# First attention of a four-part macaron block: state growth and A x V of the tile in front issued ahead of the scores, use of the state behind them

## The reference

```
qkv = x @ Wqkv_w.T + Wqkv_b ; k = k * SCALE ; g = sigmoid(gamma_raw)      # 16 heads of 16
for each position t of a sequence of 1024:
    state = g * state + v_t k_t^T          # 16 x 16 for each head
    y_t   = state @ q_t
x = x + y @ out_w.T + out_b
```

## Time and profile before

| | us |
|---|---|
| median of 3 runs | 2789.87 |
| profiled execution, whole time | 2792.29 |
| profiled execution, span | 2790.3 |
| first attention, from about 564 to 1018 | 454 |
| TensorE busy in these 454 | 407.6 |

### The profile page before, as it was taken

The page is one execution under the profiler, slowest core; times in us unless marked ns, Lnnn a source line. Parts: engine busy times, 40 slices in busy tenths (PEclk is TensorE's granted clock), DMA queues, the critical chain, the costliest instruction groups (busy, mean ns, idle before and its releaser), DMA issues.

```text
span 2790.3 us, 75964 instructions
## 1 busy us (share of the span) xinstructions
PE 2565.9 (92%) x31464; PEld 2148.2 (77%) x31464; DVE 1795.8 (64%) x4190; ACT 1369.6 (49%) x2281; POOL 1146.1 (41%) x1382
## 2 busy tenths in 40 slices
PE   4999999989989969999999899988999999969998
PEld 3888788777777757877887688877888888848887
DVE  7887788445655558888876466554656656545554
ACT  4444444244444424434443577765444544427776
POOL 5555555333333325555554333311443443453332
PEclk9999999899999989999999999999999999989999
DMA  5000000000110010000000000000000000000001
GB/s 174 1 6 1 1 1 1 1 18 22 22 22 22 22 46 1 1 1 1 1 1 1 17 1 1 1 9 19 17 17 18 17 17 18 19 1 23 31 31 38
DMA packets 67557, 45.85 MB, mean 16 GB/s; under 512 B 13184, under 2 KB 66192, under 8 KB 67216
## 3 DMA queue, kind: packets, MB, share of 16 engines
q1 hardware_dynamic: 67216, 41.00, 5.4%
HBM read 15.78 MB, written 8.40 MB: 9 GB/s over the span
## 4 chain that ended last, share of the span: by engine, by line
PE 25%; issue 13%; POOL 11%; DVE 8%; ACT 6%; SPq 0%; DMA 0%; POOLq 0%; DVEq 0%; ACTq 0%
PE ps L591 5%; PE ps L46 3%; PE ps L48 3%; PE ps L47 3%; PE ps L246 2%; PE ps L1373 2%; ACT XN L234 2%; DVE st L203 2%; POOL rs L219 2%; PE ps L1374 2%; POOL a1pry L1943 2%; POOL a1pry L1945 2%; POOL a1l L1931 2%; ACT gHf L1413 2%; DVE XTL L256 1%
## 5 line engine op out<-in xcount | busy, mean ns | idle before, releaser
L591 PE MATMUL ps<-WDT,fHT 128*128 128x256 f32 (+1 forms) x1536 | 386.0, 394 | 8.7 <-ACT fHT L642 8.7
L591 PEld LDWEIGHTS ps<-WDT,fHT 128*128 128x128 f32 (+1 forms) x1536 | 283.4, 192 | 82.4 <-issue 42.8
L1438 DVE TENSOR_TENSOR gHl<-gHf,gHh 128x512 fp32r<-128x512 f32 x256 | 180.6, 707 | 256.3 <-ACT gHh L1417 256.1
L720 POOL TENSOR_TENSOR fV<-fH,frc 128x704 f32<-128x704 f32 x128 | 178.3, 1393 | 339.3 <-DVE frc L709 339.3
L46 PE MATMUL ps<-WGH,XTH 128*128 128x512 f32 (+1 forms) x768 | 312.6, 407 | 2.4 <-DVE XTL L256 1.4
L48 PE MATMUL ps<-WGL,XTH 128*128 128x512 f32 (+1 forms) x768 | 289.0, 376 | 0.0
L47 PE MATMUL ps<-WGH,XTL 128*128 128x512 f32 (+1 forms) x768 | 288.5, 376 | 0.0
L1388 PE MATMUL ps<-W2T,gHh 128*128 128x256 f32 x1024 | 257.8, 285 | 0.0
L1390 PE MATMUL ps<-W2T,gHl 128*128 128x256 f32 x1024 | 255.1, 281 | 0.0
L234 ACT ACTIVATE XN<-X,nb,rs 128x256 f32<-128x256 f32 x384 | 198.8, 589 | 69.0 <-POOL nb L223 69.0
L1373 PE MATMUL ps<-XTH,W1T 128*128 128x512 f32 x512 | 208.9, 408 | 18.9 <-DVE XTL L256 16.4
(11 more groups left out here) (225 smaller groups left out, 6386.6 us busy)
## 6 DMA issues: line engine op xcount, KB each, us to landing
X<-in_x SPq DMA_DIRECT2D x16, 512.0 KB, 8.9
a0vp<-a0vt SPq DMA_DIRECT2D x256, 32.0 KB, 1.9
a1vp<-a1vk SPq DMA_DIRECT2D x256, 32.0 KB, 2.2
out<-X SPq DMA_DIRECT2D x16, 512.0 KB, 2.9
tws<-in_w SPq DMA_DIRECT2D x2, 1024.0 KB, 7.6
WN<-in_wgu SPq DMA_DIRECT2D x3, 384.0 KB, 6.1
a0km<-in_wqkv SPq DMA_DIRECT2D x2, 384.0 KB, 3.2
a1pry<-in_aw SPq DMA_DIRECT2D x1, 768.0 KB, 4.9
```

Source lines behind the costliest of these rows:

```text
L591: h = pe.matmul(down, HT[n % 2][0:m, c, :], WDT[0:m, c, :], start=(c == 0), stop=(c == 5))
L1438: dve.tensor_tensor(Hl[m % 8][:, :], Hf[m % 4][:, :], Hh[m % 8][:, :].bitcast(F32), ALU.subtract).then_inc(s_hl, 1)
```

## The change

Tile `n` on PE was v(n), S(n), E(n-1), V(n-1), G(n), O(n-2). It becomes v(n), G(n-1), V(n-1), S(n), E(n-1), O(n-2). G thus moves one tile later in the numbering, V moves ahead of S, and E stays behind S. Since V is now the first to write bank 6, its matmuls start the group and E's end it; V waits for ACT's copy of the tile in front (`s_ye`) and ACT's copy waits for both V and E (`s_av` and `s_it`). The ring follows the new order. On DVE the state updates of tile `n-1` stand ahead of the decays of tile `n`. In tile 0 only v and S remain, and the wait for the end of the feed-forward (`s_xd`) stands in tile 1.

```
@@ slots0
             for n in range(NT + 2):
                 if n < NT:
-                    yield from [("v", n), *[("s", n, q) for q in range(4)]]
-                    if n % 8 < 7:
-                        yield ("u", n)
+                    yield ("v", n)
+                if 0 < n <= NT and (n - 1) % 8 < 7:
+                    yield ("u", n - 1)
+                if n < NT:
+                    yield from [("s", n, q) for q in range(4)]
@@ attn0_pe: enter, values
             def enter(m):
 
-                if m:
-                    pe.wait_ge(s_ye, m)
...
-                                              start=(k == 0 and (h == 0 or m % 8 == 0)), stop=False,
-                                              skip_group_check=True)
+                                              start=False, stop=True, skip_group_check=True)
...
             def values(m):
+
+                if m:
+                    pe.wait_ge(s_ye, m)
...
-                                          a0A[m % 2][:, 256 * q + c:256 * q + c + 64], start=False, stop=True,
-                                          skip_group_check=True)
+                                          a0A[m % 2][:, 256 * q + c:256 * q + c + 64],
+                                          start=(h == 0 and k == 0), stop=False, skip_group_check=True)
@@ attn0_pe: the loop over tiles
+                if n == 1:
+                    pe.wait_ge(s_xd, NT)
+                if 0 <= m < NT:
+                    grow(m)
+                    values(m)
                 if n < NT:
                     scores(n)
-                if n == 0:
-                    pe.wait_ge(s_xd, NT)
                 if 0 <= m < NT:
                     enter(m)
-                    values(m)
-                if n < NT:
-                    grow(n)
@@ attn0_act
                 if m >= 0:
                     act.wait_ge(s_av, m + 1)
+                    act.wait_ge(s_it, entered(2 * m + 1))
@@ attn0_dve
                 i, j = n // 4, n % 4
+                if 0 < n <= NT:
+                    state(2 * n - 2)
+                    if (n - 1) % 8 < 7:
+                        state(2 * n - 1)
                 if n < NT:
                     decay(n)
-                    state(2 * n)
-                    if n % 8 < 7:
-                        state(2 * n + 1)
```

## The result

Thirteen runs of the changed kernel gave 2800.94 to 2815.93 us with a median of 2812.35; thirteen of the kernel before, on the same chips, 2782.69 to 2801.63 with a median of 2793.47. The ratio is 1.0067, with a 95% interval of 1.0054 to 1.0080: the change makes the kernel 0.67% slower, some 19 us. The forecast was 2795, +5 us, with a range from 2783 to 2806. The sign was right, the size was not.

A forecast was written before the change was run, and what follows sets the result against it. Chains over ACT and POOL, not PE, were taken as the bound. Boundaries +10.4, absorption -5.2, start -1, end +1 gave +5.2 us on 2792.29, so 2797.5; less 2.4 to the median, 2795, range 2783 to 2806.

The forecast's parts named there:

- G's waits go, V's and S's come: PE's waits: G's for POOL gone, V's for the DMA from 2.9 to 20 us or more, S's some 10 us.
- The chain at an ordinary boundary, +0.74 us: Tiles 47 to 49: S waits 0.75 us, V 1.0, then V 1.1; the chunk gets 0.74 us longer.
- L: Time from the end of `Vt` to the landing of its DMAs; taken as 4.1 us, low 3.7, high 5.7.
- The clock at nothing: TensorE's granted clock: no term in the sum; half clock after the new waits only in a rival of chance 0.12.
- A half should be absorbed afterwards: The 14 chunks: half of 0.73 us a chunk, lost to single PE events, absorbed; -5.2 us, ends 0 and -10.
- The start, -1 us: Tile 0: K's transposes no longer stand behind G's 3.86 us wait, but V(0) waits for its DMAs; -1 us.
- The end, +1 us: Tiles 60 to 63, no projection behind O: S and E now stand behind V's DMA waits; +1 us.
- the new waits cost clock: Rival, chunk boundaries: three shorter waits lower the clock in 10 more boundaries, +10 on top of +5, 2807; chance 0.12.
- PE becomes the bound: Rival: V hardly waits for DMAs, G's waits go, S's 0.75 us comes at 15 chunks; -18 us, 2774; chance 0.12.
- 2790: Rival of no change: same chain, L 3.7, more lost time absorbed; +4.8 less 7, -2 us; chance 0.24.
- Issue early, wait late: V's DMAs: the change reverses this rule; its page's 2.0 us fixed cost would give L 3.9, total +2.4 us.
- DVE's move at nothing: DVE's state updates ahead of decays: priced at nothing, since S and V (1.7 us) cover the two updates.

The follow-up runs named there:

- the version at 2767 us: Changed kernel with bias additions behind `Vt` and `KP` of the `j = 0` tile, V behind S and E after `j = 3` tiles and at both ends: 2766.87 us, 0.9904.

## Why the prediction was wrong in size

- **G's waits go, V's and S's come.** Right: G 32.4 to 0.5 us, V 6.9 to 36.8, S 11.3 for ACT's `a0km`. "20 us or more" for V was a lower bound that said little; two waits of 1 us at 15 boundaries make 30.
- **The chain at an ordinary boundary, +0.74 us.** Right, step by step: 0.74, 0.85 and 0.97 us of waiting, `XN` 2.2 and `Vt` 7.0 us behind the K bank, chunk 27.9 us. L was 3.7 us in this chunk where 4.1 was taken; over the 14 tiles with `j = 1` it was 3.7 to 5.2, 4.3 in the mean. Undisturbed chunks take 27.1 to 27.4 us before and 27.8 to 27.9 after.
- **The clock at nothing.** This step failed. The sum (+10.4 - 5.2 - 1 + 1) has no term for the granted clock; more half clock stood only in a rival of 0.12. The runs showed 51.2 us of half clock in the stage in place of 23.9, and PE busy 11.6 us longer for the same records, against 6.9 us of added idle time, which is near the +5 of the forecast. The new waits stand on PE itself, and with useless matmuls in them half clock went to 10.2 us and 9 to 12.5 us came back, with not one dependency taken away.
- **"A half should be absorbed afterwards", -5.2 us.** The measured total hides this term under the clock, but by the profiles it was near. Of the 14 chunks the seven without half clock take 28.33 us in the mean, against 27.87 for the ten without it before: +0.46 us a chunk, where 0.74 less 0.37 was forecast. That is 6.4 of the 12.7 us of these chunks; the other 6.3 are that seven of them met half clock (30.06 us in the mean) and not four. The version with three useless matmuls, whose chunks have no half clock, has 28.31 us in the mean. These are estimates from one profile of each kernel.
- **The start, -1 us.** Failed, +3.5, in the larger part by the same term: 3.0 of the 4.5 us missed came back with useless matmuls in the wait. V(0)'s wait for its DMA (3.87 us) was foreseen; that S(1), E and what follows then run at half clock (10.2 us from 569.9) was not. With PE kept running there, tiles 0 to 2 took 16.94 us, near the 16.45 of before.
- **The end, +1 us.** +2.2: V waits 0.8 to 1.9 us at four of the last five places (in tiles 60, 61, 63 and behind the last tile). Of the last one:

```profile
1026.03 0.74 PE L970 MATMUL ps<-a0A,a0vp 128*32 128x64 f32 x32 [1.01 <-issue]
```

- **The rivals.** The one called "the new waits cost clock" had the missing mechanism, and at 2807 came nearest. It was given 0.12 because of its condition: a wait of V over the 1.4 us that G had, L above 4.5. The trace after does not bear that out. In the chunks half clock followed V's waits of 1.25 to 2.05 us at seven boundaries, at L of 4.1 to 4.9, three of them under 1.4 us; it did not follow those of 1.43, 1.61, 1.87 and 2.43 us, the last with L at 5.2. "PE becomes the bound" came true in the run without DMAs alone: it gave -18, the chip gave -38, and it needs the transfer to be free.
- **Two sizes in the working.** The rivals' 2774, 2790 and 2807 are counted from the profiled 2792.3 and the forecast from the median, 2.4 us lower, so they stand 2.4 us too high beside it. And in the prediction's last estimate of L, 1.8 us and about 2.0 us make 3.8 rather than 3.9, by which its total would be +1.0 rather than +2.4. Neither changes the outcome. The median before was 2793.47 over thirteen runs and not 2789.87, so 3.6 of the 17 us between 2795 and 2812.35 are no fault of the sum.
- **Issue early, wait late.** The rule that the prediction cited against the change (the Trainium skill, DMA: Bandwidth & Descriptors, section "Rules for kernel authors") is borne out: the same four DMAs cost 5 to 7 us where V waits late and 57.6 where it waits early.
- **DVE's move at nothing.** Right in the changed kernel, where E never waits. With V behind, the cover is gone and E waits 5.3 us for `a0S`.

What stays open is why half clock follows a wait of V of 1.25 us at tile 52 and not one of 2.43 at tile 41. The length of the wait alone does not decide it, and no run here isolates what does.

## What to carry to other kernels

When a wait moves from one instruction to another, ask what the late thing is, not who stands in front of it: here G, V and S took turns in standing for 32 to 37 us at chunk boundaries, behind POOL, four DMAs, ACT and DVE. Moving four bias additions off the chain to `Vt` was worth 21 to 25 us in the new order and 10 to 11 in the old one, without touching PE's order. Read the slack of each operand before moving its reader forward, tile by tile: the reader can move where the slack is and stay where it isn't, which is what the version at 2767 us does. And give the clock a term of its own when new stalls come to TensorE: here what followed them at half clock cost more (11.6 us) than the added standing itself (6.9 us).

## What the runs showed of the hardware

**A state update on VectorE takes three times as long beside GpSimd.** The same instruction in the two kernels:

```profile
L1134 DVE SCALAR_TENSOR_TENSOR a0S<-a0S,a0GQ,a0tmp 128x32 f32<-128x32 f32 x224 | 92.9, 455 | 4.0
```

in the changed one, and before:

```profile
L1131 DVE SCALAR_TENSOR_TENSOR a0S<-a0S,a0GQ,a0tmp 128x32 f32<-128x32 f32 x224 | 51.0, 269 | 3.9
```

The timeline of VectorE in the changed kernel shows when:

```profile
714.40 1.29 DVE L1134 SCALAR_TENSOR_TENSOR a0S<-a0S,a0GQ,a0tmp 128x32 f32<-128x32 f32 x2
...
720.94 1.24 DVE L1134 SCALAR_TENSOR_TENSOR a0S<-a0S,a0GQ,a0tmp 128x32 f32<-128x32 f32 x2
...
722.35 0.41 DVE L1134 SCALAR_TENSOR_TENSOR a0S<-a0S,a0GQ,a0tmp 128x32 f32<-128x32 f32 x2
```

At 714.40 POOL runs the bias additions (714.20 to 717.00), at 720.94 `Vt` and `KP` (720.83 to 722.13), and at 722.35 nothing: about 0.6 us an update beside POOL, 0.2 alone. By the means of the two kernels the new order puts more of the updates where POOL works. The Trainium skill (SBUF — State Buffer, section "Who interferes with whom") says that a VectorE instruction with two SBUF inputs contends with a GpSimd instruction that reads SBUF. These rows agree: the updates get longer, and POOL's instructions keep their 0.6 to 0.7 us. Here it lay under V and S; it would count where E follows at once.

**Half clock behind short waits.** It followed waits of V of 1.25 to 2.05 us in the midst of work at seven boundaries, and none of the waits under 1.25 us, but not every longer one. Between the two kernels PE's busy time in the stage grew by 11.6 us for the same instructions, its idle time by 6.9.
